# Ranks of 106,250 graph edges by source block and by spline cell: found in one pass ahead of the scatter, or column by column inside the scatter's stage

## What is computed

```python
edge_index = jnp.stack([src, dst])
h = jnp.maximum(_layernorm(x, axis=-1), 0.0)
x = x + _L0_gnn_ref(h, edge_index, edge_attr_3, ...)   # Gaussian mixture weights of edge_attr
h = jnp.maximum(_layernorm(x, axis=-1), 0.0)
x = x + _L1_gnn_ref(h, edge_index, ...)                # two mean aggregations
h = jnp.maximum(_layernorm(x, axis=-1), 0.0)
x = x + _L2_gnn_ref(h, edge_index, edge_attr_3, ...)   # spline convolutions: weights by cell of edge_attr
h = jnp.maximum(_layernorm(x, axis=-1), 0.0)
x = x + _L3_gnn_ref(h, edge_index, ...)
```

## Time and profile before

| | us |
|---|---|
| Median of 3 runs | 10750.1 (10743.76 to 10757.82) |
| The profiled execution, its own time | 10742.9 |
| Span in its profile | 10741.1 |
| Stage one | 0 to 305.2 |
| Stage two | 305.2 to 1402.9 |
| Mean granted TensorE clock over the span | 0.619 of 2.4 GHz |

### The profile page before, as it was taken

The page is one execution under the profiler, slowest core; times in us unless marked ns, Lnnn a source line. Parts: engine busy times, 40 slices in busy tenths (PEclk is TensorE's granted clock), DMA queues, the critical chain, the costliest instruction groups (busy, mean ns, idle before and its releaser), DMA issues. The chain is left out here.

```text
span 10741.1 us, 165184 instructions
## 1 busy us (share of the span) xinstructions
PE 5932.8 (55%) x43331; PEld 4877.0 (45%) x43332; DVE 5442.2 (51%) x9592; ACT 2152.9 (20%) x5870; POOL 6471.3 (60%) x6754
## 2 busy tenths in 40 slices
PE   5300046666577776666555666655555455555665
PEld 1200025555377774444444555524444444445555
DVE  8300065555555556888786555661111333367645
ACT  0000014444233331111101322001111111123140
POOL 0677727777477776777650416537777777765241
PEclk8555578778655556888755756575555555556575
DMA  9970002222333331111193747665000111115655
GB/s 367 200 73 5 5 31 83 82 82 82 70 104 106 104 104 49 53 53 54 38 181 91 223 141 222 157 72 43 14 13 12 24 28 28 28 41 186 158 210 124
DMA packets 1315038, 1004.15 MB, mean 93 GB/s; under 512 B 893879, under 2 KB 1157291, under 8 KB 1305919
## 3 DMA queue, kind: packets, MB, share of 16 engines
q1 hardware_dynamic: 924062, 547.87, 23.3%
q0 software_dynamic: 225216, 279.29, 8.3%
q10 hardware_dynamic: 165600, 175.13, 5.4%
HBM read 495.57 MB, written 546.44 MB: 97 GB/s over the span
## 5 line engine op out<-in xcount | busy, mean ns | idle before, releaser
L2618 POOL DMA_INDIRECT msg<-msg,idx x1792 | 1743.1, 973 | 592.4 <-issue 532.6
L1017 POOL DMA_INDIRECT run_rows<-rec,idx x544 | 599.1, 1101 | 1120.5 <-ACT rec L995 992.5
L2448 POOL DMA_INDIRECT cell<-rec,idx x944 | 932.3, 988 | 504.4 <-issue 279.3
L2168 POOL DMA_INDIRECT cell<-rec,idx x944 | 975.0, 1033 | 407.8 <-issue 286.3
L1830 POOL DMA_INDIRECT rec_d<-rec,idx x880 | 909.1, 1033 | 456.0 <-issue 266.5
L407 POOL DMA_INDIRECT rec_r<-sc_rec,sc_idx x832 | 816.2, 981 | 580.2 <-ACT sc_rec L398 306.9
L2598 PE MATMUL ps<-w_stn,hft 128*128 x1792 | 594.1, 489 | 405.8 <-ACT hft L2552 401.9
L2385 PE MATMUL ps<-h_rows,oht 128*128 x1888 | 450.9, 403 | 537.4 <-ACT oht L2392 537.0
L281 PE MATMUL ps<-mark,column 128*128 128x416 bf16 (+2 forms) x454 | 117.5, 374 | 1095.2 <-DVE mark L212 1092.6
L2598 PE MATMUL ps<-w_conv,hft 128*128 x1792 | 436.8, 425 | 501.2 <-ACT hft L2552 501.2
L975 PE MATMUL ps<-planes,hot 128*128 x8704 | 535.8, 230 | 313.7 <-ACT rec L995 193.3
(11 more groups left out here) (425 smaller groups left out, 14604.8 us busy)
## 6 DMA issues: line engine op xcount, KB each, us to landing
loc<-loc_s SPq DMA_DIRECT2D x68, 2048.0 KB
got<-run_rows SPq DMA_DIRECT2D x472, 224.0 KB
got<-rec_d SPq DMA_DIRECT2D x236, 416.0 KB
rec_d<-padd ACTq DMA_DIRECT2D x4, 12480.0 KB
rec_d<-padd ACTq DMA_DIRECT2D x4, 12064.0 KB
cin<-cell SPq DMA_DIRECT2D x224, 136.0 KB, 2.2
cell<-rec,idx POOLq DMA_INDIRECT x1888, 2.5
loc<-loc_d ACTq DMA_DIRECT2D x118, 256.0 KB, 3.5
```

The costliest lines, as they stand in the source:

```text
L1017: nc.gpsimd.indirect_dma_start(out=out, out_offset=bass.IndirectOffsetOnAxis(ap=idx[:, u, m % HU:m % HU + 1], axis=0), in_=rec[:, m, :], i ...
L2168: nc.gpsimd.indirect_dma_start(out=cells, out_offset=bass.IndirectOffsetOnAxis(ap=idx[:, n, g:g + 1], axis=0), in_=rec[:, n, g, :], in_off ...
L2448: nc.gpsimd.indirect_dma_start(out=cells, out_offset=bass.IndirectOffsetOnAxis(ap=idx[:, n, g:g + 1], axis=0), in_=rec[:, n, g, :], in_off ...
L2618: nc.gpsimd.indirect_dma_start(out=msgs, out_offset=bass.IndirectOffsetOnAxis(ap=idx[:, n, g:g + 1], axis=0), in_=msg[:, n, g, :], in_offs ...
```

## The change

Stage one no longer ranks. For each bin DVE still makes one mark (now in a ring of four), and PE counts it with eight matmuls whose stationary operand is a slice of 104 columns of the mark and whose moving operand is a column of ones. From the totals DVE makes the bins' starts (`base_r`, `base_c`) and the maps. The keys are kept as f32 rows `key_r`, `key_c`, and `away` is a large number where an edge is padding.

Stage two finds the ranks. DVE and PE go through the columns in 208 batches of G = 4 columns, in 52 groups of R = 4 batches, for both orders. For each batch and order DVE makes a 0/1 tile of 4 columns x 64 bins (`rank_hot`), PE makes 14 matmuls on it (`rank_batch`), and DVE adds the running starts, advances them, multiplies by the 0/1 tile and reduces (`rank_position`). After each group of 16 columns `rows` turns positions into RROWR and RROWC. ACT's feed waits for the group (`placed`). The layer norm and all that hangs on it comes on DVE and PE after the last group, and ACT's square root stands between turn 17 and turn 18 of the feed (LATE = 18). The core of the diff:

```diff
+        def tally_marks(v, c, key, bins):
+            for b in range(bins):
+                if b >= 4:
+                    v.wait_ge(c["counted"], b - 3)
+                nc.vector.tensor_scalar(c["marks"][b % 4][:, :], key, iota_f[:, b:b + 1], None, ALU.is_equal).then_inc(c["marked"], 1)
...
+        def tally_pe(pe, c, bins):
+            M, bank = c["cols"] // MQ, c["bank"]
+            for b in range(bins):
+                pe.wait_ge(c["marked"], b + 1)
+                for q in range(MQ):
+                    mm = nc.tensor.matmul(ps[0:M, bank, b * MQ + q:b * MQ + q + 1], c["marks"][b % 4][:, q * M:(q + 1) * M], ones_b[:, 0:1],
+                                          start=True, stop=True)
+                mm.then_inc(c["counted"], 1)
...
+        def rank_hot(v, s, key, k, m):
+            v.wait_ge(s["s_rank"], k + 1)
+            nc.vector.tensor_tensor(s["hot"][:, m, :, :], bcast(iota_f[:, 0:CELLS].unsqueeze(1), [P, G, CELLS]),
+                                    bcast(key.unsqueeze(2), [P, G, CELLS]), ALU.is_equal).then_inc(s["s_hot"], 1)
+        def rank_position(v, s, to, k, m):
+            at, sel = ps[:, s["bank"], 0:(G + 1) * CELLS].rearrange("p (g x) -> p g x", x=CELLS), s["sel"][:, m % 2, :, :]
+            v.wait_ge(s["s_rank"], k + 1 + R)
+            v.wait_ge(s["s_next"], k + 1)
+            nc.vector.tensor_tensor(sel, at[:, 0:G, :], bcast(s["upto"][:, :].unsqueeze(1), [P, G, CELLS]), ALU.add).then_inc(s["s_with"], 1)
+            v.wait_ge(s["s_with"], k + 1)
+            nc.vector.tensor_tensor(s["upto"][:, :], s["upto"][:, :], at[:, G, :], ALU.add).then_inc(s["s_next"], 1)
+            nc.vector.tensor_tensor(sel, sel, s["hot"][:, m, :, :], ALU.mult).then_inc(s["s_sel"], 1)
+            v.wait_ge(s["s_sel"], k + 1)
+            nc.vector.tensor_reduce(to, sel, AX.X, ALU.add).then_inc(s["s_pos"], 1)
+        def rank_batch(pe, s, k, m):
...
+            for g in range(G + 1):
+                for b in range(g):
+                    mm = nc.tensor.matmul(at[:, g, :], ones_b[:, :], hot[:, b, :], start=(b == 0), stop=(g == G and b == G - 1))
+                if g < G:
+                    mm = nc.tensor.matmul(at[:, g, :], before_b[:, :], hot[:, g, :], start=(g == 0), stop=True)
...
-        def scatter_feed(act, s, row, rec, i, first):
+        def scatter_feed(act, s, placed, row, rec, i, first):
             for n in range(2):
                 j = i * (2 * GN) + n * GN
+                act.wait_ge(placed, 4 * i + 2 * n + 2)
...
-                    sort_pe(pe, srt["r"], 50)
-                    sort_pe(pe, srt["c1"], CELLS)
+                    tally_pe(pe, srt["r"], NB)
+                    tally_pe(pe, srt["c1"], CELLS)
...
+                    scatter_feed(act, rings, s_placed, rec_n[:, :, RROWR], rec_n[:, :, :], 0, True)
+                    with act.Fori(1, LATE) as i:
+                        scatter_feed(act, rings, s_placed, rec_n[:, :, RROWR], rec_n[:, :, :], i, False)
                     act.wait_ge(s_var, 1)
                     nc.scalar.activation(std[:, :], var[:, :], ACT.Sqrt).then_inc(s_std, 1)
-                    with act.Fori(1, NTURN) as i:
+                    with act.Fori(LATE, NTURN) as i:
...
+                    with pe.Fori(0, NG) as i:
+                        for n in range(R):
+                            rank_batch(pe, ranks_r, i * R + n, n)
+                            rank_batch(pe, ranks_c, i * R + n, n)
...
+                    hots(0, 0, 0)
+                    with v.Fori(0, NG) as i:
+                        for n in range(R):
+                            hots(i * R + n + 1, i * STEP + (n + 1) * G, (n + 1) % R)
+                            rank_position(v, ranks_r, raw_r[:, n * G:(n + 1) * G], i * R + n, n)
+                            rank_position(v, ranks_c, raw_c[:, n * G:(n + 1) * G], i * R + n, n)
+                        rows(i, ranks_r, raw_r, ints_r, s_row_r, RROWR, TILES_N)
+                        rows(i, ranks_c, raw_c, ints_c, s_row_c, RROWC, TC)
```

More of the change, by code:

```diff
@@ L146, in build @@
         pad2, zpad = sb_in(ctx, "pad2", [P, 2, F2 + 4]), sb_in(ctx, "zpad", [P, 2 * (F1 + 1)])
+        before_b, ones_b = (sb_in(ctx, k, [P, P], BF16) for k in ("before_b", "ones_b"))
         tick = nc.alloc_semaphore("tick")
@@ L353, in sort_own, with tally_shared @@
             return s
+        GONE = 15.0e6
+        def tally_shared(c, cols):
+            s = dict(cols=cols, marks=[sb_in(c, f"mark{n}", [P, cols], BF16) for n in range(4)])
+            s["counts"], s["totals"] = sb_in(c, "counts", [P, MQ * CELLS]), sb_in(c, "totals", [P, CELLS])
+            for k in ("endt", "nt", "st"):
+                s[k] = sb_in(c, k, [P, CELLS])
+            s["tot_i"] = sb_in(c, "tot_i", [P, CELLS], I32)
+            s["cmp"] = sb_in(c, "cmp", [P, MQ, CELLS])
+            s["tb"], s["up"] = sb_in(c, "tb", [P, MQ]), sb_in(c, "up", [P, MQ])
+            s["d0"], s["d1"] = sb_in(c, "d0", [P, MQ], I32), sb_in(c, "d1", [P, MQ], I32)
+            return s
@@ new lines, in tally_own @@
+        def tally_own(c, shared, bank):
+            s = dict(shared)
+            s["bank"] = bank
+            s["tbi"], s["tba"], s["tbb"] = (sb_in(c, k, [P, MQ], I32) for k in ("tbi", "tba", "tbb"))
+            s.update({k: sem_in(c, k) for k in ("marked", "counted", "kept", "summed", "mapped", "stored")})
+            return s
+        def tally_marks(v, c, key, bins):
[3 more added lines that the diff above has]
+                nc.vector.tensor_scalar(c["marks"][b % 4][:, :], key, iota_f[:, b:b + 1], None, ALU.is_equal).then_inc(c["marked"], 1)
@@ new lines, in tally_dve @@
+        def tally_dve(v, then, c, bins, base):
+            M, bank = c["cols"] // MQ, c["bank"]
+            v.wait_ge(c["counted"], bins)
+            nc.vector.tensor_copy(c["counts"][0:M, 0:bins * MQ], ps[0:M, bank, 0:bins * MQ]).then_inc(c["kept"], 1)
+            then(nc.vector.memset(c["totals"][:, :], 0.0))
+            v.wait_ge(c["summed"], 1)
+            then(nc.vector.tensor_reduce(c["totals"][:, 0:bins], ps[:, bank + 1, 0:bins * MQ].rearrange("p (b q) -> p b q", q=MQ),
+                                         AX.X, ALU.add))
+            sort_bases(then, c, c["totals"][:, :])
+            then(nc.vector.tensor_scalar(base[:, :], c["st"][:, :], float(P), None, ALU.mult))
@@ new lines, in tally_pe @@
+        def tally_pe(pe, c, bins):
+            M, bank = c["cols"] // MQ, c["bank"]
+            for b in range(bins):
[4 more added lines that the diff above has]
+                mm.then_inc(c["counted"], 1)
+            pe.wait_ge(c["kept"], 1)
+            nc.tensor.matmul(ps[:, bank + 1, 0:bins * MQ], ones[0:M, :], c["counts"][0:M, 0:bins * MQ], start=True, stop=True).then_inc(c["summed"], 1)
@@ L437, in build @@
         padr = sb_in(nat, "padr", [P, TURN, RW])
+        key_r, key_c = sb_in(nat, "key_r", [EP, EJ + G]), sb_in(nat, "key_c", [EP, EJ + G])
+        away = sb_in(nat, "away", [EP, EJ])
+        base_r, base_c = sb_in(nat, "base_r", [P, CELLS]), sb_in(nat, "base_c", [P, CELLS])
         with ExitStack() as c:
@@ L451, in build @@
             sg_b = sb_in(c, "sg_b", [P, KG * KD])
-            shared = sort_shared(c, EJ)
-            srt = {k: sort_own(c, shared) for k in ("r", "c1")}
+            shared = tally_shared(c, EJ)
+            srt = {k: tally_own(c, shared, bank) for k, bank in (("r", 0), ("c1", 2))}
             s_src, s_dst, s_att, s_tables, s_out, s_blank, s_io, s_c, s_pads, s_x, s_fill, s_k = (sem_in(c, n) for n in (
@@ L539, in _ @@
                     then(nc.vector.tensor_scalar(before[:, :], iota_f[:, :], lane_c[:, 0:1], None, ALU.is_gt))
-                    sort_consts(then, shared)
+                    then(nc.vector.tensor_copy(before_b[:, :], before[:, :]))
+                    then(nc.vector.memset(ones_b[:, :], 1.0))
                     n_load = 16 * len(PARTS)
@@ L572, in build @@
             h0, hT = sb_in(c, "h0", [P, NB, C]), sb_in(c, "hT", [C, NP])
-            d, sq = sb_in(c, "d", [P, NB, C]), sb_in(c, "sq", [P, NB, C])
+            d, sq = (h1[:, q * NB * C:(q + 1) * NB * C].rearrange("p (b f) -> p b f", f=C) for q in range(2))
             m, var, std, r = (sb_in(c, n, [P, NB]) for n in ("m", "var", "std", "r"))
@@ L576, in build @@
             left = sb_in(c, "left", [P, 2, XW])
+            NG, LATE = EJ // STEP, 18
+            ranks_r, ranks_c = rank_rings(c, 0, base_r), rank_rings(c, 1, base_c)
+            raw_r, raw_c = sb_in(c, "raw_r", [P, STEP]), sb_in(c, "raw_c", [P, STEP])
+            ints_r, ints_c = ([sb_in(c, n, [P, STEP], I32) for n in ("pos_i", "lane", "tile")] for _ in range(2))
+            s_row_r, s_row_c, s_placed = (sem_in(c, n) for n in ("row_r", "row_c", "placed"))
+            assert NG * STEP == EJ and GN == STEP
             s_k, s_var, s_std, s_h, s_tr, s_hT, s_w, s_xg, s_split, s_root, s_filled = (sem_in(c, n) for n in (
```

58 lines of the change are left out of this document (49 added, 9 removed).

## The result

| | before | after |
|---|---|---|
| median of 10 runs each, one chip | 10746.93 us (10732.90 to 10767.89) | 10785.30 us (10769.69 to 10817.78) |
| ratio | | 1.0039, 95% interval 1.0026 to 1.0052 |
| profiled execution, its span | 10741.1 us | 10816.0 us |

The change makes the kernel 38 us slower by the medians, 28 to 56 us by the interval. The profiled execution of the changed kernel took 10817.8 us, the slowest of its ten. So its rows are used for where things stand, and the size of the change is taken from the medians.

A forecast was written before the change was run, and what follows sets the result against it. It took stages with different limits: stage one ended by DVE and the `rec_d` fill within 9 us, stage two by POOL's scatters. -8 + 15 + 34 = +41 on 10750.1 gives 10791, range 10756 to 10875.

The forecast's parts named there:

- Stage one, -8: End of stage one: the `rec_d` fill still ends it near 294.3, so stage two begins at about 297; gain 8 us.
- The rival with 0.05: Stage one: the fill doesn't end it, so the kernel gains 130 to 190 and gives back 49: about 10640; chance 0.05.
- DVE idle from 110 to 170 on: Stage one: with ranking gone, DVE finishes near 110, or 170 with dearer matmuls, then idles under the fill.
- The fourth rival: Stage one: PE's 904 narrow matmuls take over 0.28 each, so DVE's tally passes the fill; chance 0.03.
- The first scatter, +15: Start of stage two: POOL's first scatter comes 18 us after the barrier instead of 2.7, a loss of 15 us.
- The batch, 3.42: Ranking loop of stage two: one batch, both orders, takes DVE 3.42 us, counted from rows of operations.
- `rows` and the branch, 1.3 for a group: Ranking loop: eight small operations of `rows` and the loop's end cost 1.3 us for each group of 16 columns.
- rival 1: Ranking loop slower: 0.10 more on each of four waits a batch, turn 18 at 887, +82, 10873; chance 0.20.
- Contention, 35 us: Stage two: DVE operations with two SBUF inputs delay 576 scatters by 0.061 each, 35 us, bounds 0 and 58.
- in step: Ranking loop: POOL's reads land just after a DVE operation boundary, so contention costs scatters nothing.
- The overlap of contention and root: Turn 18 starts at the later of 770 plus contention (c) and 800 (root ready), after the barrier; taken as 805.
- The sum: Whole kernel: -8 + 15 + 34 = +41, giving 10791.

The follow-up runs named there:

- experiment 4: Changed kernel with the `rec_d` fill moved from ACT in stage one to SP in stage two: 10616.23, ratio 0.9874 to the kernel before.
- experiment 5: Kernel before the change with the `rec_d` fill moved to SP in stage two: 10755.66, ratio 1.0008 to the kernel before.
- experiment 1: Changed kernel with ACT's square root in front of turn 20, not 18: 10752.98, ratio 1.0005 to the kernel before.
- experiment 7: Changed kernel with DVE's loop over 52 groups written as 26 turns of two groups: 10789.59, ratio 1.0039 to the kernel before.
- experiment 2: Changed kernel with bin numbers and `bin_sel` in PSUM, so no 256-wide loop operation has two SBUF inputs: 10793.39, ratio 1.0037 to the kernel before.

## Why the prediction was right, point by point

The forecast was 10791 and the median is 10785.3; +41 against the measured +38. The mechanisms held, and two of the sizes did not, with opposite signs.

- **Stage one, -8: right.** -8.5 (305.16 to 296.68), with the fill at 404 GB/s to 295. Experiments 4 and 5 show both halves of the argument: without the fill stage one ends at 129, and with DVE's old chain the fill's absence is worth nothing. The rival with 0.05 (faster, 10640) was priced within 24 us: 10616 when its condition was made true.
- **DVE idle from 110 to 170 on: right**, at 126. The narrow matmuls were dearer than I had costed them (DVE waited 26.5 us in all for the tally, L384 for `ps` of L404), which an idle of 170 us hides. The fourth rival never came near.
- **The first scatter, +15: right.** 314.71 against the expected 315, 18.0 behind the barrier.
- **The batch, 3.42: right to the hundredth**, since each of its ten steps came from a row of the same width.
- **`rows` and the branch, 1.3 for a group: wrong, 1.85.** I took the eight small operations at 0.14 and little for the branch. Missing were the 0.14 to 0.17 in front of L773, twice a group, and the branch's 0.35. L773 writes to an address that hangs on the loop's register, behind a wait, and that may be the reason; no run took the two apart. I had the number in hand, the 0.43 of L1961 in the earlier trace rows, and used it only to weigh a rival on the ten operations of a batch. 52 x 0.55 = 29 us. With it the sum of the prediction closes: 1.5 + 208 x 3.42 + 52 x 1.85 = 809, and 6 for POOL's hold (below) give 815, where the ranks did end (1112.1). I had 789. This is a piece of rival 1, which had a chance of 0.20 and a price of +82 (its four waits of 0.10 make 0.40 a batch and not 0.42, so +78).
- **Contention, 35 us: wrong, 17.** 0.030 for each of the 576 scatters in place of 0.061. The row it came from (L1830 beside operations of 0.68) had longer operations to be held by; the new ones are 0.42. The size also isn't fixed by the code: the same loop has 0.029 in experiment 4, 0.021 in experiment 1 and, with the branch halved, 0.018 in experiment 7. The bound below (0, "in step") was as near as the value I took. DVE was held for some 0.12 a group (15.67 while POOL scattered, 15.54 while it stood), 6 us where I had 8, and nearly all of it in the eight small operations of `rows` and not in the wide ones.
- **The overlap of contention and root: right, and it is why the two errors nearly cancelled.** I had turn 18 at the later of 770 + c and 800, with c deciding. In fact POOL was through at 789 (1085.3 in the trace) and the root was ready only for 825. The larger of the two moved from 805 to 825, so turn 18 was mis-sized by 20, though one term was 18 too large and the other 26 too small. "From an end of the ranks of 794 on each microsecond of DVE is one of the kernel" was met: experiment 7 shows it at 6.1 for 6.1, experiment 1 gives the stand back, and experiment 2 shows that c was worth nothing then.
- **The sum.** By the rows of this trace it is -8.5 + 15 + 52 = +59 at the last scatter, where I had +41, and the medians say +38. **The 21 us between the last two are in part open.** Some 8 of them may be the profile before: its 3.42 in front of the 226th scatter (experiment 5) makes its stage two shorter than what the other traces have. In eight of the nine kernels that were traced on the first chips, what lies behind the last scatter took 2 to 20 us less than in the profile before, though its lines are the same, and the ninth is the changed kernel with its own 22 more. A second pair of traces on the first chip would have told whether stage two of the kernel before takes longer in most executions than in the profiled one, or the later stages take less. So the total is right to 6 us with a stage two whose loss in the traces is 18 larger than forecast, or some 10 if the pause of the profile before is the exception. That part is luck.
- **On another chip the prediction is wrong.** Rival 1 happens there in a size that my range has no place for (+552). Nothing in the one trace of before pointed to it.

## What to carry to other kernels

Before work is taken off an engine, look for the second chain that ends the stage: here a fill issued elsewhere ended within 9 us of DVE, so 176 us of relief were worth 8.5. The moves of the work and of the fill gain nothing one by one (+38 us, and +10 with an interval that holds 0) and 1.3% together. Where a loop is moved under another engine's, ask which single instruction needs the whole loop's result (the variance, and the root in ACT's feed queue behind it), and put it behind everything that doesn't need it: one number here was worth nearly the whole loss. Count the small operations and the branch by their own rows, and ask what a lockstep of three engines does when one hand-over is late: on the second chip it turned 38 us into 552. Whether more margin would have paid there wasn't run.

## What the runs showed of the hardware that I had not expected

- **A scatter is held by a DVE operation with two SBUF inputs, but briefly:** 18 to 30 ns in the mean beside four operations of 0.42 in 3.42 us, against 100 if its read fell evenly. With one input in PSUM it is 0, for a group of 15.75 us in place of 15.67. By the Trainium skill (SBUF — State Buffer, Who interferes with whom) the first of the two holds the shared ports for its whole instruction, and the prediction's estimate from that was 58 us; the trace has 17.
- **A saturated DMA does not slow scatters.** They took 0.97 to 1.0 us beside 361 GB/s. What is longer beside it are the pauses of POOL that recur every 112 scatters. They last 1.7 us where the DMA engines are nearly idle, 5 to 6 beside the fill of `rec_d` in stage two, and 3.4 to 11.5 beside the fills of `cell1` and `msg1`.
- **A branch of a DVE loop shows as an idle 0.35** with one group a turn. With two groups a turn it is 0.48 at the branch and 0.05 between the groups, so halving the branches gave back 0.17 for each that went, and not 0.35. The last of the small operations, behind a wait and with a register in its address, starts 0.14 to 0.17 late.
- **Two chips can differ by 14.5% on one program** (10747 and 12306), and by more in what a change does to it (1.004 and 1.045). On the slower one a group of the lockstep of PE and DVE took 28 to 31 us in place of 15.5 as long as POOL issued indirect DMAs.
